# Two experts per token through routing, scatter and fetch, or all sixteen experts for every token with a gate: a Trainium2 encoder step

## The reference

```python
# 1. tokens: 1024 grid points per image, 8 sampled neighbours each (4 corners per neighbour)
q_feat  = bilinear_sample(feature_map, ref)                       # -> queries, and offsets by a small MLP
sampled = bilinear_sample(feature_map, ref + offsets)             # [b, 1024, 8, 64]
keys, values = sampled @ W_k.T, sampled @ W_v.T                   # attention of a point over its 8 samples
h = concatenate([tokens, txt], axis=1)                            # [32, 1152, 64]
# 2. causal attention over the 1152 tokens of an image, one head of 64
h = h + attn(layernorm(h))
# 3. mixture of experts: 16 experts of 64 -> 128 -> 64, the two best by the gate
gate_logits = x @ gate_w + gate_b
topk_vals, topk_idx = top_k(gate_logits, 2); topk_w = softmax(topk_vals)
h1 = relu(einsum('bsh,ehf->bsef', x, w1) + b1)
expert_out = einsum('bsef,efh->bseh', h1, w2) + b2
y = x + sum(topk_w * take(expert_out, topk_idx))                  # layer norm of y, added to h
```

## Time and profile before

| | us |
|---|---|
| three timed executions | 4560.54, 4563.92, 5620.5 |
| their median | 4563.92 |
| profiled execution, span from first to last instruction | 6851.9 |
| one period of the profiled execution (13 of them) | 370 to 448 |
| PE, DVE, ACT, POOL busy in the profiled execution | 4265.1, 3165.0, 2222.4, 3077.1 |

### The profile page before, as it was taken

How to read it: one execution, slowest core, us unless ns; L and a number is a source line. 1 busy time by engine, 2 the same in 40 slices (tenths; PEclk the granted TensorE clock), 3 DMA queues, 4 the chain that set the end, 5 groups by cost and what they waited for, 6 DMA issues and landing times.

```text
span 6851.9 us, 83914 instructions
## 1 busy us (share of the span) xinstructions
PE 4265.1 (62%) x26592; PEld 3681.7 (54%) x26592; DVE 3165.0 (46%) x10220; ACT 2222.4 (32%) x5378; POOL 3077.1 (45%) x3089
## 2 busy tenths in 40 slices
PE   3566765657566575665766667565765757656664
PEld 2555655646455464654656556454654646545543
DVE  1455445354454534545354544534545454544521
ACT  1333332323333332332333323333333333322321
POOL 2554454444534445354454544445344444545331
PEclk9777777777767776786777767777777777767765
DMA  6754443635536354353545536254353545433122
GB/s 194 216 154 136 145 135 115 177 96 157 148 103 189 86 174 119 118 165 94 175 118 160 144 106 190 84 176 119 118 164 93 175 113 152 138 106 89 54 59 67
DMA packets 938637, 911.33 MB, mean 133 GB/s; under 512 B 121306, under 2 KB 822362, under 8 KB 938072
## 3 DMA queue, kind: packets, MB, share of 16 engines
q1 hardware_dynamic: 805768, 598.22, 30.0%
q0 software_dynamic: 132432, 307.74, 15.5%
HBM read 583.69 MB, written 323.53 MB: 132 GB/s over the span
## 4 chain that ended last, share of the span: by engine, by line
another core or an unknown queue 31%; PE 29%; DVE 14%; issue 13%; ACT 10%; SPq 1%; DMA 1%; POOL 0%; DVEq 0%; POOLq 0%; ACTq 0%
PE ps L867 4%; PE ps L881 4%; PE ps L1024 3%; PE ps L1032 3%; PE ps L812 3%; PE ps L964 3%; PE ps L942 2%; ACT rows L1048 2%; ACT xm L1128 2%; DVE prod L1229 1%; PE ps L954 1%; PE ps L1006 1%; PE ps L823 1%; ACT kv_sb L1048 1%
## 5 line engine op out<-in xcount | busy, mean ns | idle before, releaser
L758 POOL DMA_INDIRECT gath<-table,idx x2048 | 2048.2, 1000 | 2909.6 <-issue 1211.3
L881 PE MATMUL ps<-w_kv,samp_t 128*128 128x128 f32 x4096 | 702.9, 323 | 166.6 <-issue 88.1
L867 PE MATMUL ps<-const,prod 128*128 128x128 f32 x4096 | 684.4, 322 | 168.8 <-issue 81.7
L964 PE MATMUL ps<-v_sb,probs_t 128*128 128x64 f32 x2880 | 455.2, 307 | 476.9 <-issue 223.1
L881 PEld LDWEIGHTS ps<-w_kv,samp_t 128*128 128x128 f32 x4096 | 637.0, 234 | 201.0 <-issue 130.5
L964 PEld LDWEIGHTS ps<-v_sb,probs_t 128*128 128x128 f32 x2880 | 442.9, 229 | 544.2 <-issue 303.5
L867 PEld LDWEIGHTS ps<-const,prod 128*128 128x128 f32 x4096 | 596.5, 172 | 202.7 <-issue 152.4
L774 POOL DMA_INDIRECT xs_d<-xm,row x512 | 525.9, 1027 | 392.7 <-DVE row L1229 231.6
L790 POOL DMA_INDIRECT ya<-ys_d,row x512 | 493.4, 964 | 454.4 <-DMA ys_d<-yx 268.6
L1229 DVE TENSOR_TENSOR prod<-gath,corner_w 128x1024 f32<-128x1024 f32 x512 | 619.9, 1219 | 159.3 <-remote 70.6
L942 PE MATMUL ps<-k_t,q_t 128*128 128x512 f32 (+3 forms) x960 | 479.7, 592 | 181.6 <-ACT v_sb L1048 76.5
(11 more groups left out here) (171 smaller groups left out, 6593.0 us busy)
## 6 DMA issues: line engine op xcount, KB each, us to landing
table<-rows SPq DMA_DIRECT2D x224, 1024.0 KB
fm<-in_x SPq DMA_DIRECT2D x256, 512.0 KB
wx<-w_d SPq DMA_DIRECT2D x768, 128.0 KB
gath<-table,idx POOLq DMA_INDIRECT x2048
wx<-w_d SPq DMA_DIRECT2D x64, 512.0 KB
table<-rows SPq DMA_DIRECT2D x32, 960.0 KB
xg<-xs_d SPq DMA_DIRECT2D x192, 130.0 KB
ys_d<-yx SPq DMA_DIRECT2D x192, 128.0 KB
```

The source lines that it names most:

```text
L758: pool.indirect_dma_start(out=gath[:, n % NG, p, :], out_offset=None, in_=tables[par], in_offset=bass.IndirectOffsetOnAxis(ap=idx[:, par, ...
L867: last = pe.matmul(bank(0, p * P, p * P + P), prod[h][:, (p * 2 + dx) * P:(p * 2 + dx + 1) * P], ident, is_transpose=True, start=(dx == 0) ...
L881: last = pe.matmul(bank(1, p * P, p * P + P), samp_t[n % 2][:, (4 * h + p) * P:(4 * h + p + 1) * P], w_kv[:], start=True, stop=True)
L964: last = pe.matmul(bank(7, (i % 8) * C, (i % 8) * C + C), probs_t[n % 3][:, (k % 4) * P:(k % 4) * P + P], v_sb[:, k, :], start=(k == 0), s ...
```

## The change

Every token passes all 16 experts. Per image there are 36 units: 32 of one expert and 512 grid tokens (`u % 16` is the expert, `u // 16` the half of the image) and 4 of four experts and the 128 text tokens. A unit is one layer-1 step into bank 2 (one matmul of 512 columns, or four of 128), one DVE instruction that takes relu and multiplies with the gate (`gated`, zero for the 14 experts not chosen), and one layer-2 step that adds into bank 5: two matmuls of 256 columns with 64 output partitions each, into the lower and the upper half of the partitions. After 16 units the sum is copied (ACT), turned back and joined by the gated bias (PE), and added to the tokens (DVE). The gates of an image are turned on PE, stored to DRAM as 16 rows and read back row by row, each row to all 128 partitions (72 loads of 256 KB a pair, four buffers). The weights stay in SBUF. Routing, scatters, fetches, weight and token loads, the DRAM buffers, and `combine` are gone. Scores have bank 4 alone, so that bank 5 holds the sum; attention's other tiles use banks 4, 6, 7. The order strings are all new.

```diff
-            def scatter(pair, par, j):
-            def fetch(pair, par, b, j):
...
             def expert_1(pair, par, b, u):
+                n = UNITS * b + u
...
+                else:
+                    pe.wait_ge(*h_sb.rise(pair, n))
+                if u < 2 * E:
+                    pe.matmul(bank(2), w1[0:XW, u % E, :], xt[0:XW, b, u // E * BANK:u // E * BANK + BANK],
+                              start=True, stop=True).then_inc(h_ps.sem, 1)
                     return
...
+            def expert_2(pair, par, b, u):
+                n = UNITS * b + u
+                pe.wait_ge(*h_sb.rise(pair, n + 1))
...
+                h = gated[n % SLOTS]
+                if u < 2 * E:
+                    e = u % E
+                    for half in range(2):
+                        last = pe.matmul(bank(5, 0, 2 * P)[C * half:C * half + C], w2[:, e, :],
+                                         h[:, 2 * P * half:2 * P * half + 2 * P], start=(e == 0), stop=(e == E - 1))
+                else:
+                    for m in range(4):
+                        e = 4 * (u - 2 * E) + m
+                        last = pe.matmul(bank(5, 0, P)[0:C], w2[:, e, :], h[:, m * P:m * P + P],
+                                         start=(e == 0), stop=(e == E - 1))
+                last.then_inc(y_ps.sem, 1)
...
+            def expert_gate(pair, par, b, u):
+                n = UNITS * b + u
+                h = gated[n % SLOTS]
+                dve.wait_ge(*g_in[n % SLOTS].rise(pair, 16 * (n // SLOTS + 1)))
+                dve.wait_ge(*h_ps.rise(pair, n + 1))
+                stt(h[:], bank(2), 0.0, h[:], ALU.max, ALU.mult).then_inc(h_sb.sem, 1)
...
+            def gate_load(pair, par, b, u):
+                if n >= SLOTS:
+                    sp.wait_ge(*y_ps.rise(pair, n + 1 - SLOTS))
...
+                sp.dma_start(gated[slot][:], src.unsqueeze(0).to_broadcast([P, BANK])).then_inc(g_in[slot].sem, 16)
...
-                elif n == 1:
-                    pe.wait_ge(*v_cp.rise(pair, 2 * b + 2))
-                else:
-                    pe.wait_ge(*s_rd.rise(pair, KEY_CHUNKS * b + n - 1))
+                    pe.wait_ge(*v_cp.rise(pair, 2 * b + 1))
+                else:
+                    pe.wait_ge(*s_rd.rise(pair, KEY_CHUNKS * b + n))
...
-                pe.matmul(bank(4 + n % 2, 0, m), q_t[:, i * P:(i + 1) * P], k_t[:, a:a + m],
+                pe.matmul(bank(4, 0, m), q_t[:, i * P:(i + 1) * P], k_t[:, a:a + m],
```

More of the change, by code:

```diff
@@ L459, in build @@
[L459 to L469 removed]
+        lg = sb("lg", [P, 3, ST_N, E])
+        dense = lg[:, 0]
@@ L564, in threads_of @@
                    "grid": (pair + 1, 1 - par), "gather": (pair + 1, 1 - par),
-                   "second": (pair - 1, 1 - par), "route": (pair - 1, 1 - par), "experts": (pair - 1, 1 - par),
-                   "rest": (pair - 2, par), "fetch": (pair - 2, par), "end": (pair - 2, par)}
+                   "second": (pair - 1, 1 - par), "experts0": (pair - 1, 1 - par), "experts1": (pair - 1, 1 - par),
+                   "end0": (pair - 1, 1 - par), "end1": (pair - 2, par)}
         def follow(engine, stages, k, pair, par):
@@ L1028, in expert_2, with gate_turn @@
-            def expert_2(pair, par, g):
-                pe.wait_ge(*hx_sb.rise(pair, g + 1))
-                for n in range(4):
-                    last = pe.matmul(bank(2, n * C, n * C + C), hx[:, n * P:n * P + P],
-                                     weights_of(g)[:, n, F:F + C], start=True, stop=True)
-                last.then_inc(yx_ps.sem, 1)
-            pe.wait_ge(*tables_in.rise(Pair(0), 32))
+            def gate_turn(pair, par, b):
+                pe.wait_ge(*dense_ok.rise(pair, b + 1))
+                if b:
+                    pe.wait_ge(*moe_ok.rise(pair, SUMS))
+                elif begun(pair - 1):
+                    pe.wait_ge(*moe_ok.rise(pair - 1, 2 * SUMS))
+                pe.transpose(bank(2, 0, P), dense[:, 0:QT_N].rearrange("p t e -> p (t e)"), ident)
+                pe.transpose(bank(2, P, 2 * P)[0:E], dense[:, QT_N], ident).then_inc(gt_ps.sem, 1)
```

604 lines of the change are left out of this document (215 added, 389 removed).

## The result

The changed kernel takes **5901.5 us** (median of 4 runs, 5885 to 5938) where the kernel before takes 4569.8: a ratio of 1.293, with a 95% interval of 1.288 to 1.298. The forecast was 4766, with a range of 4430 to 5100. The sign was right, the size far off. The ratios in this document leave out single executions more than 1.5% above the fastest of the same kernel, such as the 5620.5 us of the kernel before; e15's trace is of such an execution (6605 us).

A forecast was written before the change was run, and what follows sets the result against it. PE was taken as the bound of the changed kernel, 268 us of full-clock work giving 288 us a period: 4564 + 221 (13 periods) + 81 (second period) - 100 (end) = 4766 us, 4% slower, range 4430 to 5100.

The forecast's parts named there:

- The timed runs know little of the standstills: Kernel before: the stops behind POOL's bursts in the profiled execution (period 410 us) are mostly absent from timed runs.
- 271 us a timed period: Kernel before, between two exps of the offsets: 3522 us for 13 periods, 271 us each, near 250 of undisturbed windows.
- PE's full-clock need: PE work a period at 2.4 GHz: 194 us before, 194 - 44.5 + 118 = 268 us after.
- The halves overlap, a layer-2 step 0.68 us: Layer 2 on PE: matmuls into different output halves run together, 0.436 us plus 0.24 for the step's change of outputs.
- DVE 222 to 242: DVE a period after the change: 197 + 53 less 8 to 28, 222 to 242 us, staying below PE.
- Gate loads and the single bank at nothing: SP's gate loads with four buffers, and scores in one bank: no cost, covered by other PE work.
- the new period: Period after the change: PE's 268 us at 0.93 busy and full clock, 288 us, bounds 276 and 305.
- The end: From the last exp to the end: 574 us in timed terms becomes 474, a gain of 100 us.
- The profiled execution: Changed kernel's profiled span: about 6600 us, with 288 + 107 = 395 us a period, while the timed median rises.
- The halves don't overlap: Rival, layer 2 on PE: each step costs 0.43 us more, period 318, about 5230 us; chance 8%.
- gate rows come late: Rival, SP's queue: late gate loads hold up DVE, +24 us a period, about 5120 us; chance 12%.
- POOL's relief wins: Rival: fewer POOL DMAs ease timed runs, or switches hide behind waits; period 264 us, 4405 in all; chance 20%.

The follow-up runs named there:

- e15: Changed kernel with the gate instruction on 64 of 512 columns, repeat of e7: 6570 us, 0.933 of the kernel before (7019).
- e12: The kernel before, unchanged, traced where it takes about 4570 us: 4570 us, one run.
- e3: Changed kernel without the 72 gate loads a pair, DVE multiplying by a constant tile: 6569 us, 0.940 of the kernel before (7001).
- e5: The changed kernel, unchanged, on a chip where the kernel before takes 6943 us: 6556 us, ratio 0.946.
- e8: The kernel before without its 32 scatters and 32 fetches a pair on POOL: 5848 us, 0.843 of the kernel before (6943).
- e17: Changed kernel with idle PE stretches filled by extra passes and POOL waiting every four gathers: 5762 us, 0.832 of the kernel before (6941).
- e18: Changed kernel with bfloat16 experts and POOL waiting between whole gathers of eight transfers: 5750 us, 0.829 of the kernel before (6941).
- e4: Changed kernel with fewer PE columns for every second grid expert: 6392 us, 0.915 of the kernel before (7001).
- e7: Changed kernel with the gate instruction on 64 of 512 columns: 6507 us, 0.940 of the kernel before (6943).
- e14: Changed kernel with fewer PE columns for every second grid expert, repeat of e4: 6404 us, 0.911 of the kernel before (7019).
- e11: Changed kernel with bfloat16 experts and POOL waiting every four gathers: 5226 us, 1.143 of the kernel before (4573).
- e2: Changed kernel with extra PE passes in seven idle stretches of a period: 6572 us, 0.939 of the kernel before (7001).
- e13: Changed kernel with extra PE passes in seven idle stretches, repeat of e2: 6535 us, 0.932 of the kernel before (7019).
- e9: The kernel before with POOL waiting for landing after every four indirect DMAs: 6214 us, 1.358 of the kernel before (4573).
- e1: The kernel before, unchanged, traced on a chip where it takes about 7000 us: 7001 us, ratio 1.001.
- e10: Changed kernel with POOL waiting for landing after every four gathers: 5933 us, 1.301 of the kernel before (4573).

## Why the prediction missed

**Right, by its own steps.** *The timed runs know little of the standstills*: e12, 7.4 us a period. *271 us a timed period*: 262.5. *PE's full-clock need*: 193.6 before (forecast 194), 267.0 after (268), summed by the prediction's own prices over all passes (the count was right; the prices are read from the earlier trace rows). *The halves overlap, a layer-2 step 0.68 us*: 0.09 before the first pass, 0.58 behind it, 0.67. *DVE 222 to 242*: 227.3. *The gate 0.684*: 0.688. *DMA 210 us of a period*: 0.59 x 350.7 = 207. *Gate loads and the single bank at nothing*: 19.0 us of waits in all for the one, and e3; the bank was not tried alone, and PE waited under 20 us in all for maxima in the first trace. *POOL relieved*: busy 36% of the span.

**The step that failed** is the new period, "I take the best of these and full clock: 268 / 0.93 = 288 us". The time at half clock was put at nothing, though the rows showed a granted clock of 0.75 over a full period. Measured are 350.7. The 63 us too many are 47 us for 94 us a period at half clock, and 16 us of idle time beyond the 20 that 0.93 allows. The kernel before at 4570 has 48 us at half clock and 45 us of idle time in 262.5; these 69 us of slack did not take up the new work. (Idle time is here what remains of a period without passes and clock; PE's own gaps in the traces are 39 us before and 29 after.) The new work came on top of it: 350.7 - 262.5 = 88 us are 73 of passes and 23 of clock, less 8 of idle time. 13 periods: 13 x (351.0 - 288) = 819 of the 1117 us by which the sum is too low, taken against the trace's span of 5883.5.

The prediction's own rows held a better price. It took PE's busy share of 0.94 in the fullest of the calm windows as if that were work at full clock. By its own prices the 552 passes that start in the three windows are 65 us of full-clock work in 85 us, 0.77 and not 0.93; 268 / 0.77 = 348 us. The same reckoning gives 194 / 0.77 = 252 for the kernel before, the "250" that the prediction did use for the old period. Old and new period were priced by two different measures.

**The end** was mis-sized: 738 us, not 474, 264 more. I had counted the experts of three images behind the last exp; the trace has 160 grid units of L892 there, five images. Two images are 2 x 59 us of passes; and 311 us of the end are at half clock, another 155, together a little more than the 264. The first period (183, not 148) gives the last 35. 819 + 264 + 35 = 1118.

**The profiled execution** of the changed kernel was forecast at about 6600 us with periods of 370 to 420, for a chip like that of the earlier trace rows. e5 is that case: 6497 us and 385.5. The number came true, but partly by luck: the 395 were 288 us and 107 of standstills, while e5 has 267 us of passes, 62 lost at half clock and 57 idle, of which 21 are common idle time. I had seen that relief and rise belong to two kinds of conditions, but not that the timed runs of one comparison would all be of one kind.

**The rivals.** *The halves don't overlap* and *gate rows come late* both fell. *POOL's relief wins* is what happens on 7000 chips (0.946), by the mechanism of the earlier trace rows: the other engines stop there from some 5 to 10 us into a burst (e8, e17, e18). On the 4570 chip POOL stood at 240 of 262.5 us; that relief was worth something there and PE took its place is argued, not shown.

**What e4 to e7 add**: neither TensorE's nor VectorE's work alone sets the period on a 7000 chip. Work taken from PE came back as idle time and half clock (e4, e14). Whether 30 us less of either pays on a 4570 chip was not measured; e11 says that 73 us of PE give 36 there. Open are also what makes the one or the other kind of chip, and what the engines wait for in a stop. No version here beats the kernel before at 4570; on 7000 chips the changed kernel does by 5%, and e17 and e18 do by 17%.

## What to carry to other kernels

Before a sum is made in periods of timed runs, get a trace whose span is the timed one: a profile 50% above the median is of other conditions, and a change can win in the one and lose in the other. Cost old and new matmul work by one measure, full-clock work per us of window, since a busy share hides the clock. A wait of TensorE can cost far more than itself: in the changed kernel 29 us of gaps a period came with 47 us lost at half clock, and one gap of 1.32 us with a stretch of 48 us at half clock. Filling stretches with harmless passes cost nothing on 7000 chips (e2, e13), and with the stops gone came with a period 6 us shorter. Where an unbroken series of indirect DMAs stops the other engines, waiting for the transfers every four helps (e17); where it does not, and the issuing engine is nearest to its limit, the same wait cost 36% (e9), so look for waits on "remote" first.

## What the runs showed of the hardware

- Bursts of indirect DMAs, 1.25 us apart, stop PE, DVE and ACT together on three of the four chips of e1 to e18, and not on the fourth. In e1 PE is busy 0.95 in the first 2.5 us of a burst, 0.40 at 7.5 to 10, 0.21 at 20 to 30; in e12 0.84 beyond 50 us (a burst ends where two transfers start over 2.5 us apart). Bursts of four (5 us) bring no stops in the changed kernel on either kind; waits on "remote" are 67 us in e17 and none in e10.
- TensorE can be busy and stay at 1.2 GHz: 118 us at a granted clock of 0.50, with 112.6 us of PE busy, in the changed kernel's last window above, where all but 8 of 246 passes are the experts'; and 48 us in the window from 2355, where 61 of about 111 are grid units' passes. The kind of pass alone does not do it: in the twelve periods of e17 1% of the grid units' layer-1 passes and 4% of the layer-2 passes start at half clock, against 16 and 18% in the first trace. Only the text units' passes still do in e17 (36 and 55%), in a stretch of 14 to 24 us in every period with 0.5 to 1.2 us of idle time. Why was not tried.
- Two matmuls into different halves of the output partitions started 7 ns apart, 4096 passes of 256 columns in pairs at 0.26 us.
